# Interleaving score tiles and column work inside an attention cycle of one core

## The reference

```
scores = Q K^T * scale (+ mask, + bias)
attn   = softmax(scores)          # 2048 x 2048 per head, 16 heads
out    = attn V, then times W_O, added to x
```

## Time and profile before

| what | value |
|---|---|
| median of 3 runs | 3775.59 us |
| profiled execution, its own time | 3777.26 us |
| span in its trace | 3775.5 us |
| mean granted TensorE clock | 0.979 |
| attention 0, trace time 90 to 1357 us | 1267 us, PE busy 1253.94 us |
| attention 1, 1494 to 2272 us | 778 us, PE busy 750.06 us |
| attention 2, 2475 to 3752 us | 1277 us, PE busy 1262.10 us |

### The profile page before, as it was taken

One profiled execution on the slowest core, in us unless ns is written; L12 is line 12 of the kernel. 1 busy time (PEld: TensorE's weight loads), 2 busy tenths in 40 slices (PEclk: granted clock), 3 DMA queues, 4 the chain that ended last, 5 costly groups with the idle time before them and its releaser, 6 DMA issues.

```text
span 3775.5 us, 66359 instructions
## 1 busy us (share of the span) xinstructions
PE 3594.2 (95%) x24697; PEld 2100.9 (56%) x24697; DVE 2860.7 (76%) x5691; ACT 2330.0 (62%) x3981; POOL 449.4 (12%) x486
## 2 busy tenths in 40 slices
PE   5999999999999977999999997899999999999999
PEld 3555555555555533665665554355555555555555
DVE  6878878778777776777777776577777878878784
ACT  4666666666666614666666653566666666666664
POOL 2000000000000002323232321000000000001000
PEclk9999999999999988999999997899999999999999
DMA  1000000000000000000000000000000000000000
GB/s 49 8 9 10 10 9 10 9 10 10 7 10 7 15 5 3 16 14 15 16 11 16 14 13 6 19 8 9 8 13 7 10 12 8 9 8 11 7 10 15
DMA packets 43641, 43.14 MB, mean 11 GB/s; under 512 B 16210, under 2 KB 30298, under 8 KB 43066
## 3 DMA queue, kind: packets, MB, share of 16 engines
q1 hardware_dynamic: 43322, 38.88, 3.6%
HBM read 36.38 MB, written 1.69 MB: 10 GB/s over the span
## 4 chain that ended last, share of the span: by engine, by line
PE 86%; DVE 7%; ACT 2%; issue 2%; SPq 1%; DMA 1%; POOL 1%; DVEq 0%; POOLq 0%
PE ps L599 83%; DVE over L1395 1%; DVE x L1578 1%; PE ps L946 1%; DVE wexp L1395 1%; PE ps L957 1%; SPq L514 1%; DMA auxQ<-mrow 1%; DVE V L1303 0%; PE ps L885 0%; DVE stats L1291 0%; PE ps L983 0%; DVE acc L1372 0%; ACT wexp L1118 0%; SPq L470 0%
## 5 line engine op out<-in xcount | busy, mean ns | idle before, releaser
L1372 DVE TENSOR_TENSOR acc<-acc,work 128x1024 f32<-128x1024 f32 (+2 forms) x1152 | 1387.6, 1205 | 62.6 <-ACT work L1103 18.6
L599 PE MATMUL ps<-work,V 128*64 128x512 f32 (+3 forms) x5376 | 1232.9, 579 | 0.0
L599 PE MATMUL ps<-Qh,Kh 64*128 64x512 f32 (+3 forms) x2688 | 864.2, 483 | 22.6 <-DMA auxQ<-mrow 9.6
L1100 ACT ACTIVATE work<-ps 128x512 f32<-128x512 f32 (+1 forms) x1344 | 790.6, 588 | 90.7 <-PE ps L599 85.5
L1395 DVE CUSTOM_DVE_ANT_0 over<-ps,over,mpart 128x512 f32<-128x512 f32 (+3 forms) x642 | 423.3, 697 | 499.2 <-PE ps L599 491.5
L1103 ACT ACTIVATE work<-ps 128x512 f32<-128x512 f32 (+1 forms) x1344 | 795.8, 592 | 0.0
L599 PEld LDWEIGHTS ps<-work,V 128*64 128x64 f32 x5376 | 448.4, 137 | 542.0 <-issue 444.5
L599 PE MATMUL ps<-Qh,Kl 64*128 64x512 f32 (+3 forms) x2688 | 732.9, 387 | 0.0
L599 PE MATMUL ps<-Ql,Kh 64*128 64x512 f32 (+3 forms) x2688 | 728.1, 384 | 0.0
L599 PE MATMUL ps<-auxQ,auxK 64*128 64x512 bf16 (+3 forms) x2688 | 720.9, 380 | 0.0
L1085 ACT ACTIVATE over<-ps 128x1024 f32<-128x1024 f32 (+1 forms) x321 | 316.1, 985 | 575.8 <-PE ps L599 575.8
(11 more groups left out here) (193 smaller groups left out, 2903.7 us busy)
## 6 DMA issues: line engine op xcount, KB each, us to landing
rden<-inverse_sums SPq DMA_DIRECT2D x186, 128.0 KB, 2.9
auxQ<-mrow SPq DMA_DIRECT2D x384, 1.0 KB
wqk<-in_wqk SPq DMA_DIRECT2D x24, 128.0 KB, 2.5
dcomp<-rden SPq DMA_DIRECT2D x186, 2.0 KB
wv<-in_wv SPq DMA_DIRECT2D x24, 64.0 KB, 2.2
inverse_sums<-rcomp SPq DMA_DIRECT2D x93, 4.0 KB, 1.3
work<-in_mlp_w SPq DMA_DIRECT2D x1, 1024.0 KB
work<-in_c_aux SPq DMA_DIRECT2D x1, 1024.0 KB, 4.9
```

The source lines that it names most:

```text
L599: return pe.matmul(o, w, m, start=start, stop=stop, skip_group_check=True)
L1100: act.activation(work[:, 2 * e, q0:CH], ps[:, b, q0:CH], ACT.Exp, scale=L.scale)\
L1372: dve.tensor_tensor(o, o, work[:, slots[two]:slots[two] + 2, q0:CH], ALU.add).then_inc(s["acc_ready"], 1)
```

## The change

Each cycle of PE is issued in two halves. `row_block` is cut after `base` of unit 0 into `first_rows` and `second_rows`; `column_block` takes a parameter `half`. The order on PE becomes: excess 0, score tiles 0 and 1, base 0; jobs of slot 0, the first `values`; score tiles 2 and 3, base 1, excess 1; the second `values`, jobs of slot 1, jobs of slot 2. Jobs of slot 1, which stood between the two `values`, now come behind the second. No instruction is added or taken away on any engine, and no stream but that of PE is touched.

```
-                def row_block(x):
+                def first_rows(x):
...
                         pe.wait_ge(s["relu_ready"], L.NR * m + L.relus_to[u] + 1)
                         base(m, m % 2, u)
+
+                def second_rows(x):
+
+                    n, g = x // L.G, x % L.G
+                    p = n % 2
+                    tiles = 4 * x
+                    units = {sl: (m, u) for sl, m, u in L.units_in(x)}
                     scores(n, p, 2 * g + 1, 0, tiles + 1)
                     scores(n, p, 2 * g + 1, 1, tiles + 2)
...
-                def column_block(x):
+                def column_block(x, half):
...
-                    jobs(0)
-                    for half in range(2):
-                        if 0 < x <= L.G * PAIRS:
-                            n, g = (x - 1) // L.G, (x - 1) % L.G
-                            values(n, n % 2, 2 * g + half)
-                        jobs(1 + half)
+                    if half == 0:
+                        jobs(0)
+                    if 0 < x <= L.G * PAIRS:
+                        n, g = (x - 1) // L.G, (x - 1) % L.G
+                        values(n, n % 2, 2 * g + half)
+                    if half == 1:
+                        jobs(1)
+                        jobs(2)
...
                 for at in range(L.X):
                     if L.main(at):
-                        row_block(at)
-                    column_block(at)
+                        first_rows(at)
+                    column_block(at, 0)
+                    if L.main(at):
+                        second_rows(at)
+                    column_block(at, 1)
```

## The result

The changed kernel takes 4085.84 us (median of 4 runs, 4084.74 to 4087.24), the kernel before 3776.08 on the same chip. The ratio is 1.0817, 95% interval 1.0804 to 1.083: 310 us slower. The forecast was 4100 us. The page of the kernel after has a span of 4083.0 us; these are its engines and the chain that ended last, to be held against the earlier trace rows.

A forecast was written before the change was run, and what follows sets the result against it. PE, busy 95% of the span, was taken to bound the kernel. Waits of +264 us in the full layers and +80 in the causal one, less 20 for maxima rows, gave +324 and 4100 us, range 3950 to 4230.

The forecast's parts named there:

- The wait for the tops of unit 1: At the next excess 0, PE waits 1.20 us less later jobs; 8.4 plus 3.1 us a full-layer pair.
- the last link: End of unit 1's tops to the end of the next cycle's excess 0, put at 0.45 us.
- The wait for the low part: Before score tile 1, for SCB banks behind DVE's low part: 0.7 us in six cycles, 5.6 a pair.
- Full layers: Layers 0 and 2 together: waits for tops and the low part add 264 us.
- Causal layer: Layer 1: waits for tops and SCB banks add 80 us, between 20 and 150.
- The waits for the rows of maxima: Job mt comes nearer the cycle's start, so 19.6 us of waits may go whole: -20 us.
- Idle time behind the tops: Sign: PE or its weight loads idle before Kd,Qh behind DVE's mpart or mcol, over 150 us, against 29.7.
- PE's own balance: PE alone, if it never waits: +0.37 us for entering and leaving column work, -0.41 for the stagger, -0.04 a cycle.
- the stagger: Tiles 2 and 3: heads' matmuls not starting as pairs costs 0.41 us a cycle, which the change removes.
- The rival that ended faster: ACT and DVE reach unit 1 early enough, excess 0 never waits, only PE's balance counts: 3735 us; chance 0.04.
- Switches alone: No wait, but the stagger stays while column work is entered and left twice: 3880 us; chance 0.08.
- The clock: PE's idle time closes the clock gate for a tenth of 3,300 us, +165 at half weight: 4230 us; chance 0.08.

The follow-up runs named there:

- unit_early: Changed kernel with unit 1's excess and base ahead of score tiles 2 and 3, their banks swapped, ACT's Relu and POOL's cut moved likewise: 3896.15 us, ratio 1.0317.
- jobs_first: Changed kernel with jobs of slot 1 put back between excess 1 and the second values: 4102.22 us, ratio 1.0861.
- more_switches: excess_first_half with its first values cut once more, one tile going between score tiles 0 and 1: 3992.96 us, ratio 1.0573.
- excess_first_half: unit_early with excess 1 behind base 0, slot 1 jobs ahead of the second values, waiting only for tile 2's exponentials: 3906.59 us, ratio 1.0343.
- before_paired: Kernel before, with score tiles that wait for banks waiting for both heads' exponentials at once, so matmuls start as pairs: 3835.35 us, ratio 1.0147.
- whole: excess_first_half with the column work not halved but in one piece behind score tile 3: 4238.16 us, ratio 1.1226.

## Why the prediction came out right, and where it did not

**The wait for the tops of unit 1.** Right in mechanism and nearly in size. A cycle without later jobs was put at 10.01 us plus J0; the op cycles among them take 10.97 with a job of 0.87, so 10.10. The 0.09 between them is about the last link, read from a narrower product (0.45 instead of 0.56). The wait's parts are split otherwise than I said: excess 0 waits 1.04, not 1.20, and excess 1 waits 0.28 for tile 2's exponentials, which I had called free; the chain does not notice it, since ACT is still busy then. unit_early shows the cause: 1.1 us a plain cycle comes back with nothing changed but the place of unit 1 on PE, ACT and POOL, the banks of tiles 2 and 3, and the waits that go with them.

**The wait for the low part.** Said 0.7 behind a Q or K job and 1.4 with an op job ahead. Measured, tiles 0 and 1 take 2.59 and 3.19 instead of 1.85: 0.74 and 1.34. Behind cycles 0 and 4, whose first two sums are one, it is 0.40. For a pair that is 5.0 us and not 5.6. That it hangs on the end of the tops and not on the jobs' place is in the prediction's sum, and jobs_first showed it; my expectation for that run forgot it.

**Sums by layer.** Full layers: +264 - 20 said, +246 measured. Causal layer: +80 said, +61 measured, a term somewhat too large; within its bounds. The waits for the rows of maxima went from 19.6 to 4.1 us, nearly whole, as said. Idle time behind the tops was to be over 150 us: it is 160.2 for PE (29.7 before) and 390.4 for its weight loads (75.9 before); the two cover in part the same waits.

**PE's own balance.** The arithmetic holds, its use did not. A plain cycle of the kernel after takes 10.09 us; without the 1.04 at excess 0 and the 0.28 at excess 1 that is 8.77, against 8.81 before: the -0.04 of the prediction, 0.37 for the switches (0.35 in more_switches) against 0.41 for the stagger. What failed is "nothing, if PE never waits", with excess 1 put down as free. The stagger was not work that could be won back but a wait for ACT's pace, and it comes back elsewhere: as excess 1's 0.28 here and in excess_first_half, as 0.24 of tile 3 for the Relu in unit_early (9.01, so 8.77 without it), as 0.23 of excess 1 in before_paired. So a version without any wait for tops is not at -0.04 but at about +0.2 a cycle. The forecast did not depend on it, because the chain over ACT and DVE is longer than PE's work either way. The rival that ended faster did.

**Rivals.** Switches alone (3880): the stagger is gone, as the "x2" rows show, and the waits are there. The clock (4230): the granted clock stayed at 1.00 in both full layers. That number does not follow from its terms either: 4100 with 165, or with half of it, is 4265 or 4182. PE busy was to be under 92% in them and is 93 and 94%; part of that is short waits which hide in overlapping records.

No version tried beats the kernel before. That halves must lose is not shown; what is shown is that the best one here is 87 us slower, while entering and leaving column work once more in 336 cycles, 0.35 each time, comes to 118 us by itself.

## What to carry to other kernels

On an engine that is busy all the time, a step's distance to its consumer matters more than its place: count, from the moved instruction, every link on the other engines up to the first wait that comes back, and compare it with the work that is left in between. A stagger or a gap beside a wait is not a loss until the wait's releaser is shown to have time to spare. Read waits of TensorE from end to end of its matmuls; the idle column showed 0.44 of a wait of 0.71, and nothing of one of 0.28.

## What the chip showed beside it

In the causal layer of the kernel after, the mean granted clock is 0.99 where it was 1.00. In whole, where PE is busy 88% of each stage (96 to 99% before), the same layer has 0.97 and the last attention 0.99, while the first keeps 1.00. Windows of whole:

```profile
90.00:1540.00 1450.00, 1278.54 (x8483) 663.93 (x8479) 1001.91 (x1733) 836.46 (x1411) 78.31 (x58) 1.00 0.03 9
1680.00:2560.00 880.00, 770.91 (x5970) 455.18 (x5970) 573.82 (x1382) 497.70 (x916) 214.80 (x298) 0.97 0.04 13
2750.00:4210.00 1460.00, 1292.97 (x8695) 678.52 (x8696) 1004.06 (x1718) 830.27 (x1399) 80.87 (x61) 0.99 0.03 8
```

The losses are small, 3% at most in a stage. In the runs here they appear only in versions in which PE pauses more than before, but not in all of them: more_switches keeps 1.00 in the causal layer, with PE busy 754.36 of 820 us, about as much as in the kernel after. That the pauses cause them was not tested by itself, and why one stage and not another is open.
